# Attention on 32 graphs, one core: sums taken half a step earlier, output products and shares half a step later, paired negations, and the values' second copy issued from ACT's queue

## What is computed

```
q, k, v = (proj(Wq, bq), proj(Wk, bk), proj(Wv, bv))
scores = einsum('bhqd,bhkd->bhqk', q, k) * SCALE * (adj + adj)
attn = softmax(scores, axis=-1)
ctx = einsum('bhqk,bhkd->bhqd', attn, v)
out = layernorm(x + ctx @ Wo.T + bo)
```

## Time and profile before

| | us |
|---|---|
| median of 3 runs | 419.25 (416.65 to 419.89) |
| profiled execution, its time | 418.86 |
| its span | 416.3 |

### The profile page before, as it was taken

How to read it: one execution, slowest core, us unless ns; L and a number is a source line. 1 busy time by engine, 2 the same in 40 slices (tenths; PEclk the granted TensorE clock), 3 DMA queues, 4 the chain that set the end, 5 groups by cost and what they waited for, 6 DMA issues and landing times.

```text
span 416.3 us, 12182 instructions
## 1 busy us (share of the span) xinstructions
PE 382.1 (92%) x3628; PEld 291.4 (70%) x3628; DVE 386.2 (93%) x1592; ACT 361.6 (87%) x1223; POOL 249.6 (60%) x379
## 2 busy tenths in 40 slices
PE   8989999999996999999999999899999999997772
PEld 6766777777674877777777776677777777675542
DVE  4988999999997799999999999999999999999865
ACT  4699999989897798999999999889899999999560
POOL 3143557677573775748577575757758474555455
PEclk9999999999999899999999999999999999999898
DMA  8468889989988789889989888888999898888632
GB/s 272 131 173 238 236 201 254 245 237 247 244 237 234 191 223 244 244 243 251 253 237 246 241 237 235 230 242 233 248 245 248 227 232 208 219 234 183 144 105 76
DMA packets 65427, 92.29 MB, mean 222 GB/s; under 512 B 8529, under 2 KB 48722, under 8 KB 65362
## 3 DMA queue, kind: packets, MB, share of 16 engines
q1 hardware_dynamic: 47426, 66.35, 63.9%
q10 hardware_dynamic: 17936, 25.17, 18.0%
HBM read 26.22 MB, written 8.39 MB: 83 GB/s over the span
## 4 chain that ended last, share of the span: by engine, by line
DVE 33%; PE 28%; DMA 12%; SPq 11%; issue 9%; ACT 4%; POOL 1%; DVEq 0%; ACTq 0%; POOLq 0%
DVE boxes L540 15%; DVE probs L521 13%; SPq L208 9%; DMA v_boxed<-v 8%; PE ctx_bank L404 7%; PE out_bank L421 5%; PE proj_bank L333 5%; PE out_bank L351 4%; PE row_bank L264 3%; ACT probs L728 3%; DMA carried<-boxes 3%; PE turn_bank L281 2%; SPq L217 2%; DVE stats L567 1%; DVE low_top L530 1%
## 5 line engine op out<-in xcount | busy, mean ns | idle before, releaser
L728 ACT ACTIVATE probs<-probs,low_top 128x256 f32<-128x256 f32 x512 | 254.6, 504 | 12.1 <-DVE low_top L530 12.1
L521 DVE CUSTOM_DVE_ANT_0 probs<-row_bank,adj_rows 128x256 f32<-128x256 f32 x512 | 187.4, 414 | 6.7 <-PE row_bank L264 5.9
L540 DVE STREAM_TRANSPOSE boxes<-probs 128x1536 f32<-128x1536 f32 x62 | 109.6, 1768 | 0.0
L333 PE MATMUL proj_bank<-xt_parts,w_parts 128*128 128x512 f32 x360 | 99.2, 411 | 0.0
L728 ACT ACTIVATION_READ_ACCUMULATOR probs<-probs,low_top 128x1 f32 x512 | 99.1, 194 | 0.0
L333 PEld LDWEIGHTS proj_bank<-xt_parts,w_parts 128*128 128x128 f32 x360 | 62.9, 188 | 30.5 <-issue 19.9
L404 PE MATMUL ctx_bank<-carried,v_boxed 128*32 128x256 f32 x744 | 61.9, 392 | 18.3 <-DMA v_boxed<-v 12.2
L867 POOL COPY wide<-shares 128x512 f32<-128x512 f32 x32 | 19.5, 610 | 92.2 <-DVE shares L548 92.2
L264 PE MATMUL row_bank<-kq 32*128 32x256 f32 x1024 | 73.3, 400 | 0.5 <-DVE top L521 0.5
L404 PEld LDWEIGHTS ctx_bank<-carried,v_boxed 128*32 128x32 f32 x744 | 32.3, 111 | 43.4 <-issue 31.4
L264 PEld LDWEIGHTS row_bank<-kq 32*128 32x128 f32 x1024 | 46.3, 184 | 11.7 <-issue 6.4
(11 more groups left out here) (85 smaller groups left out, 461.1 us busy)
## 6 DMA issues: line engine op xcount, KB each, us to landing
carried<-boxes SPq DMA_DIRECT2D x248, 192.0 KB, 3.9
xt<-in_x_t SPq DMA_DIRECT2D x32, 256.0 KB, 3.5
adj_rows<-in_adj ACTq DMA_DIRECT2D x32, 256.0 KB, 4.8
xr<-in_x ACTq DMA_DIRECT2D x32, 256.0 KB, 3.8
v_boxed<-v SPq DMA_DIRECT2D x124, 64.0 KB, 3.0
out<-result ACTq DMA_DIRECT2D x31, 256.0 KB, 5.3
w_whole<-in_wk ACTq DMA_DIRECT2D x2, 128.0 KB, 3.7
w_whole<-in_wq SPq DMA_DIRECT2D x1, 256.0 KB, 4.3
```

The lines of the kernel that those rows point to most:

```text
L333: last = nc.tensor.matmul(proj_bank[:], w_parts[:, a, which, t, c * P:(c + 1) * P], xt_parts[:, pair % 2, b, t, :], start=(half_ == 0 and ...
L521: last = nc.vector.tensor_tensor_reduce(probs[:, h % RING, t * S:(t + 1) * S], row_bank[j][:, t * S:(t + 1) * S], adj_rows[:, (g // 2) % 2 ...
L540: nc.vector.transpose(boxes[:, n % BOXES].rearrange("p a h (f q) -> p (h f) a q", q=D), probs[:, first:first + BOXED, :].rearrange("p h (f ...
L728: last = nc.scalar.activation(tile, tile, ACT.Exp, bias=low_top[:, g % 2, J * c + j, t:t + 1], accum_out=sums[:, g % 2, t, j * T + c:j * T ...
```

## The change

- **ACT**: `carry_v` moves from SP's list to ACT's: for graph 0 in slot 2 of step 0, and for graph g+1 in slot 6 of step g, behind that slot's `exp`. `copy_v(g+1)` goes from slot 3 to slot 5, ahead of `move_turned(2g)`. `copy_inverse` is now of graph g-2 and stands ahead of the step's first `exp`. `load_masks` goes from slot 2 to slot 4. `store` is of graph g-5, not g-4. The values' landing is told by four semaphores instead of two.
- **PE**: in a step, `project_out` is of graph g-3 and stands with `turn_shares(g-2)` ahead of `weigh_v(g-2)` in the first half; `project_v(g+1)` moves from the first half to the end of the second, ahead of `turn_probs(2g)`. `project_out` and `turn_shares` leave the second half.
- **DVE**: the eight `lower_top` of a step become four `lower_tops`, each for two heads; the first of a group stands behind its third `reduce_rows`, the second behind its fourth. `add_residual` and `row_stats` are of graph g-3, `aggregate` of g-4; `scale_context(g-2)` goes from the step's middle, ahead of `box(2g-1)`, to behind it.
- **POOL**: `make_scale` and `normalise` are of graph g-4, and the steps' slots are arranged anew.
- Behind the last step more is left over: an output product, a set of shares, an aggregate and a normalisation.

```diff
@@ SP @@
-            def carry_v(n):
-                sp.wait_ge(v_ready, n + 1)
-                wait(sp, ctx_made, n - 3)
-                for j in range(J):
-                    sp.dma_start(v_boxed[j::J, (n // 2) % 2, n % 2].rearrange("p t e -> p (t e)"),
...
                 if 0 < g <= LAST:
                     carry_boxes(2 * g - 1)
-                if 0 <= g + 1 < LAST:
-                    carry_v(g + 1)
@@ PE @@
-                if g < B:
-                    rows(2 * g)
+                rows(2 * g)
                 if is_pair(ahead):
                     for half_ in range(2):
                         project_kq(ahead, 2 * (g % 2), half_)
                 if g == 1:
                     make_bias()
+                if is_graph(g - 3):
+                    project_out(g - 3)
                 if is_graph(g - 2):
+                    turn_shares(g - 2)
                     weigh_v(g - 2)
-                if is_group(2 * g - 1):
-                    turn_probs(2 * g - 1)
-                if is_graph(g + 1):
-                    project_v(g + 1)
-                if is_graph(g):
-                    rows(2 * g + 1)
+                turn_probs(2 * g - 1)
+                rows(2 * g + 1)
                 if is_pair(ahead):
                     for half_ in range(2):
                         project_kq(ahead, 2 * (g % 2) + 1, half_)
-                if is_graph(g - 1):
-                    turn_shares(g - 1)
-                if 0 <= g - 2 < LAST:
-                    project_out(g - 2)
-                if 0 <= g < LAST:
+                if is_graph(g + 1):
+                    project_v(g + 1)
+                if g < LAST:
                     turn_probs(2 * g)
@@ DVE @@
+            def lower_tops(n, half_):
+
+                g, place = n // T, J * (n % T) + 2 * half_
+                dve.wait_ge(rows_used, J * n + 2 * half_ + 2)
+                nc.vector.tensor_reduce(low_top[:, g % 2, place:place + 2, :], top[:, g % 2, place:place + 2, :].unsqueeze(3),
+                                        AXIS.X, ALU.max, negate=True).then_inc(top_ready, 2)
...
                 for j in range(J):
                     reduce_rows(n, j)
-                    if j > 0:
-                        lower_top(n, j - 1)
+                    if j == 2:
+                        lower_tops(n, 0)
                     if j == 1 and n % T == 0 and n > 0:
                         divide(n // T - 1)
-                lower_top(n, J - 1)
+                lower_tops(n, 1)
@@ ACT @@
+            def carry_v(n):
+
+                act.wait_ge(v_ready, n + 1)
+                wait(act, ctx_made, n - 3)
+                for j in range(J):
+                    act.dma_start(v_boxed[j::J, (n // 2) % 2, n % 2].rearrange("p t e -> p (t e)"),
+                                 v[D * j:D * (j + 1), (n // 2) % 2, n % 2].rearrange("p t e -> p (t e)")
+                                 ).then_inc(v_in[n % 4], 16)
...
+                    if s == 0 and is_graph(g - 2):
+                        copy_inverse(g - 2)
                     if is_group(n):
                         exp(n, j)
...
-                    if s == 2 and is_graph(g + 2):
+                    if s == 2 and g == 0:
+                        carry_v(0)
+                    if s == 6 and 0 <= g + 1 < LAST:
+                        carry_v(g + 1)
+                    if s == (4 if g > 0 else 2) and is_graph(g + 2):
                         load_masks(g + 2)
                     if s == 1 and is_group(2 * g - 1):
                         move_turned(2 * g - 1)
+                    if s == 5 and is_graph(g + 1):
+                        copy_v(g + 1)
                     if s == 6 and is_graph(g):
                         load_x(g)
-                    if s == (3 if g > 0 else 5) and is_graph(g + 1):
-                        copy_v(g + 1)
```

More of the change, by code:

```diff
@@ L102, in build @@
         biases_in = sem("biases_in")
-        stored, v_in = ([sem(f"{name}{n}") for n in range(2)] for name in ("stored", "v_in"))
-        x_in, adj_in, carried_in = ([sem(f"{name}{n}") for n in range(4)] for name in ("x_in", "adj_in", "carried_in"))
+        stored = [sem(f"stored{n}") for n in range(2)]
+        x_in, adj_in, v_in, carried_in = (
+            [sem(f"{name}{n}") for n in range(4)] for name in ("x_in", "adj_in", "v_in", "carried_in"))
         xt_in = [[sem(f"xt_in{n}_{t}") for t in range(T)] for n in range(2)]
@@ L229, in _ @@
                     load_x_t(pair, t)
-            carry_v(0)
             def step(g):
@@ L277, in turn_probs @@
                 wait(pe, moved, n)
-                wait(pe, inverted, n // 2)
+                wait(pe, inverted, (n + 1) // 2 - 1)
                 for t in range(T):
@@ L362, in turn_shares @@
                 else:
-                    pe.wait_ge(moved, 2 * g + 2)
+                    pe.wait_ge(moved, min(2 * g + 3, 2 * LAST))
                 for half_ in range(2):
@@ L373, in weigh_v @@
                 if g < LAST:
-                    pe.wait_ge(v_in[g % 2], 64 * (g // 2 + 1))
+                    pe.wait_ge(v_in[g % 4], 64 * (g // 4 + 1))
                 if g == 0:
@@ L497, in _ @@
                 step(g)
-            for c in range(T):
-                for j in range(J):
-                    turn_last(c, j)
+            turn_shares(LAST - 1)
+            for j in range(3):
+                turn_last(0, j)
+            project_out(LAST - 2)
+            for c, j in ((0, 3), (1, 0), (1, 1)):
+                turn_last(c, j)
             weigh_v(LAST - 1)
+            for j in (2, 3):
+                turn_last(1, j)
             turn_shares(LAST)
@@ L671, in step @@
                     nc.vector.tensor_copy(bias[:], ctx_bank[:, 0:E]).then_inc(bias_ready, 1)
-                if 0 <= g - 2 < LAST:
-                    scale_context(g - 2)
+                if is_graph(g - 3):
+                    add_residual(g - 3)
                 if is_group(2 * g - 1):
                     box(2 * g - 1)
[L676 to L682, removed]
+                if is_graph(g - 4):
+                    aggregate(g - 4)
+                if is_graph(g - 2):
+                    scale_context(g - 2)
+                mask_group(2 * g + 1)
+                if g < LAST:
                     box(2 * g)
-                if 0 <= g - 2 < LAST:
+                if is_graph(g - 3):
                     for t in range(T):
-                        row_stats(g - 2, t)
+                        row_stats(g - 3, t)
             for g in range(B):
                 step(g)
-            for c, j in ((0, 2), (0, 3), (1, 0), (1, 1), (1, 2)):
-                move_last(c, j)
+            aggregate(LAST - 3)
+            for j in (2, 3):
+                move_last(0, j)
+            add_residual(LAST - 2)
+            for j in (0, 1):
+                move_last(1, j)
+            for t in range(T):
+                row_stats(LAST - 2, t)
+            scale_context(LAST - 1)
             divide(LAST)
+            move_last(1, 2)
             aggregate(LAST - 2)
-            scale_context(LAST - 1)
             for half_ in range(2):
@@ L811, in step @@
                     n, j = 2 * g + s // J, s % J
+                    if s == 0 and is_graph(g - 2):
+                        copy_inverse(g - 2)
                     if is_group(n):
                         exp(n, j)
-                    if s == 0 and 0 <= g - 4 < LAST:
-                        store(g - 4)
+                    if s == 0 and is_graph(g - 5):
+                        store(g - 5)
                     if s == 0 and g == 0:
@@ L823, in step @@
                         move_turned(2 * g - 1)
+                    if s == 5 and is_graph(g + 1):
+                        copy_v(g + 1)
                     if s == 6 and is_graph(g):
                         load_x(g)
-                    if s == (3 if g > 0 else 5) and is_graph(g + 1):
-                        copy_v(g + 1)
                     if s == (3 if g > 0 else 4) and is_pair(ahead):
                         read_kq(ahead, 2 * (g % 2) + 1)
-                    if s == 3 and is_graph(g - 1):
-                        copy_inverse(g - 1)
+                    if s == 2 and g == LAST:
+                        copy_inverse(LAST - 1)
                     if s == 5 and 0 <= g < LAST:
@@ L841, in _ @@
             move_last(1, 3)
-            store(LAST - 3)
+            store(LAST - 4)
             copy_inverse(LAST)
@@ L845, in _ @@
                 high_last(half_)
-            for n in (LAST - 2, LAST - 1):
+            for n in (LAST - 3, LAST - 2, LAST - 1):
                 store(n)
@@ L924, in step @@
                 for s in range(H):
-                    if s == 0 and is_graph(g - 1):
+                    if s == 0 and g % 2 == 1 and is_pair(g // 2 + 2):
+                        cut_x(g // 2 + 2, 1)
+                    if s == 1 and is_graph(g - 1):
                         spread_shares(g - 1)
-                    if s == 1 and g % 2 == 1 and is_pair(g // 2 + 2):
-                        cut_x(g // 2 + 2, 1)
```

(9 more changed lines are left out.)

2 lines of the change are left out of this document (removed).

## The result

The changed kernel takes 524.84 us (median of 6 runs, 521.89 to 527.27) against 416.7 us for the one before in the same rounds: a ratio of 1.258 (95% interval 1.2515 to 1.2649). The direction was forecast; the forecast of 437 us and its range to 446 us were far too low. (The title speaks of sums taken half a step earlier. The diff leaves `weigh_v(g-2)` in the first half of its step, only behind `project_out` and `turn_shares`.)

The account below looks back on a forecast made before the run. ACT was taken to become the bound, at 12.70 us a step: 27.0 + 2 + 30 x 12.70 + 25.4 + 1 = 436.4 us of span, 439 us by the sum, taken as 437; own range 429 to 446 us.

Parts of the forecast that it names:

- the cover of 1.46 us: ACT's work in hand when the first issue starts: `move_turned` and the `exp` of slot 6, between `copy_v` and slot 7.
- the five: Four `carry_v` issues and `load_x` on ACT's queue before slot 7's `exp`: 2.4 us plus 0.58, 3.0 us together.
- A load of 0.33 us in the midst of an issue of SP: ACT's load during SP's 2.77 us issue stayed short, so no waiting for SP's issues was put in the sum.
- The rival with dearer issues: ACT's issues wait for SP's, 0.3 us more each: 4.2 us, stall 2.7, steps 13.9, 472 us in all; chance 0.07.
- The rule beside it, of a lock held by one queue at a time: The descriptor-making unit is locked for one queue at a time; cited for a still dearer issue, not put in the sum.
- ACT's step is then 11.15 + 1.55: ACT's work of 11.15 us plus its stall ahead of slot 7 of 1.55 gives a step of 12.70 us.
- `copy_inverse` fills most of the later start: On ACT, a group's first `exp` can start about 0.8 us later; `copy_inverse`, 0.46 us, fills most of that.
- The pairing: On DVE, two heads' negations in one instruction save 0.14 us a group, 0.28 a step: 11.64 becomes 11.36 us.
- PE's waits for blocks vanish, 11.6 us a step without the stall: PE's wait ahead of `weigh_v`, 18.2 us in all, goes; PE's floor stays 11.56 us, steps near 11.6 without stall.
- Ends: Outside the 30 steps: 2 us added in step 0 for two `carry_v`, 1 us behind the last step.
- the cheap issue: ACT's issues cost 0.335 us each, PE bounds at 11.56 us, steps of 11.65, 405.5 us in all; chance 0.15.
- the bounds: Issue prices on ACT from 0.335 to near 1.0 us per set's one issue: stall 0.4 to 1.95, ACT 11.55 to 13.1 us.

Follow-up runs that it names:

- experiment 1: The changed kernel with the values' second copy issued from SP again, as before the change: 422.31 us, 1.0129 of the kernel before.
- experiment 2: The kernel before with only the values' second copy moved to ACT's queue, slot 6, `copy_v` staying in slot 3: 437.59 us, 1.0483.
- experiment 10: The changed kernel with the burst in the same slot 6 but of graph g, whose `copy_v` was done a step earlier: 448.62 us, 1.0786.
- experiment 9: The changed kernel with SP's block copies moving 128 of each row's 1536 bytes, same number of issues: 493.52 us, 1.1877.
- experiment 7: The changed kernel with the values' four issues on ACT taken apart, one each in slots 6, 7, 1 and 2: 425.13 us, 1.0194.
- experiment 3: The changed kernel with DVE's `divide` moved behind the whole mask, values still issued from ACT: 509.21 us, 1.2157 of the kernel before.
- experiment 11: The changed kernel with the values' issues on ACT one each in slots 6, 7, 1 and 2, and negations for each head: 408.19 us, 0.9823.

## Why the prediction was right and wrong

- **Direction and place: right.** ACT's queue was named as what decides, with the wait behind `copy_v`, the cover of 1.46 us, and the idle time ahead of slot 7 put down to "issue". The cover is 4.59 - 3.14 = 1.45 us. Experiments 1, 2 and 10 show that this is the cause.
- **The length of the issues: the larger failed step.** The sum took 3.0 us for the five; 4.54 us were measured in the step shown (212.32 to 216.86). The first two took about what was predicted, 0.50 and 0.67 us in the mean for 0.47 and 0.60; the third and fourth 1.27 and 1.24 us in the mean, `load_x` 0.90 in the median in place of 0.58. The mean stall was 3.31 us a step in place of 1.55: 1.8 us of the missing 2.9 us a step (15.57 - 12.70). The prices were SP's own, taken while ACT's queue carried little; that the changed order puts the burst beside SP's blocks wasn't considered. A load of 0.33 us in the midst of an issue of SP was read as proof that the two don't touch. Experiment 9 shows that they do. The rival with dearer issues, 4.2 us for the five, was nearer in size, but its 0.3 us more for each had no row behind it. The rule beside it, of a lock held by one queue at a time (the Trainium skill, "Perfetto Trace Analysis", section "DMA Instruction — HWDGE"), no run here confirms as the cause: in experiment 7 issues beside one of SP were short. That the other queue's bytes matter is all that experiment 9 tells.
- **"ACT's step is then 11.15 + 1.55": the other failed step, in how the terms are added.** ACT's work and its stall were taken for the whole step. With the measured 3.3 us that rule gives 14.5 us and some 490 us in all, not 525. What stood behind `exp` 7 was listed as `box`, `turn_probs` and `read_kq`; `divide` was left out, though it waits for the eighth `exp` in the middle of DVE's masks. DVE then can't run ahead, `exp` 4 waits for it, and `copy_v`, which starts the burst, waits for `exp` 5. ACT's waits for DVE and PE are the missing 1.0 us a step; in experiment 3 the one for DVE is gone, and the step is 0.6 us shorter. By the loop, 10.83 us (15.42 - 4.59) plus the issues, the predicted 3.0 us would have given 13.8 us a step and some 470 us. So either failure alone puts the time above the range.
- **"`copy_inverse` fills most of the later start": wrong for the second group.** It stands ahead of `exp` 0. `exp` 4 has nothing ahead of it and waits 0.93 us in experiment 1. The pairing was booked as a gain of 0.28 us a step. DVE's work did fall, by 0.2 us a step after the change (11.68 to 11.47 us), but the pairing costs 13 us in the new order and 7 in the old.
- **PE's waits for blocks vanish, 11.6 us a step without the stall: right in kind.** 18.2 us became 0.9, and 1.4 in experiment 11, where no stall hides them. That run, with neither burst nor pairing, has steps of 11.60 us.
- **Ends.** 2 us were added at the start, 4.7 were found; 1 at the end, 1.2 were found. (The sum of 405.5 us for the cheap issue leaves out the 2 us; nothing hangs on it.)

The range held no case in which the stall comes back around: its highest rival needed a dearer issue, and the bounds moved only the issue's price, never the rule by which the terms are added.

## What to carry to other kernels

When a wait or a stall is put on an engine's list, follow what it releases until the chain comes back to where it began; if it comes back, the step can't be shorter than the way around, whatever idle time the engines have. In this kernel a DMA issue on a computing engine was free only while that engine had more in hand than the issue lasted. So place the issues singly, and put no set of them behind a wait for a result that the same engine has just made. Fewer instructions on the busiest engine are no gain if the first result comes later to an engine that has no work meanwhile.

## What the runs showed of the hardware

The length of an issue on ACT's queue rose with what SP's queue had to move: the set of four took 3.77 us beside full blocks and 2.83 us beside blocks of a twelfth of the bytes, while cutting the values' own bytes to a sixteenth gave 3.48 us. Why the third and fourth issue of experiment 7 take 0.95 and 1.02 us, though only 7 and 8 of 29 stand beside an issue of SP, while the first two stand beside one each time and take half as long, stays open.

PE's clock fell where PE had come to idle. The window rows of the two steps show 0.94 and 0.89 of the full clock after the change, against 1.00 before. Here PE had been idle for 2.44 us, waiting for `copy_inverse`; the 16 products of one group take 2.09 us right behind that wait and 1.15 us later in the step. The windows of these two stretches show a granted clock of 0.50 and 1.00 (third number from the end), its levels of 1.2 and 2.4 GHz:

```profile
203.70:206.80 3.10, 3.03 (x20) 1.94 (x20) 3.00 (x7) 3.10 (x12) 1.27 (x1) 0.50 0.25 85
210.50:213.10 2.60, 2.56 (x22) 2.01 (x23) 2.60 (x5) 2.60 (x10) 2.25 (x6) 1.00 1.00 285
```

The slower clock can explain little of the loss: of 109 us, DVE waits for scores 4.3 us in the whole run and ACT for `proj_bank` 10.6 us. Timeline of the changed kernel, PE:

```profile
203.77 1.09 PE L270 MATMUL turn_bank<-ident,probs 128*128 128x128 f32 x4 [2.44 <-ACT inverse L739]
204.79 2.09 PE L253 MATMUL row_bank<-kq 32*128 32x256 f32 x16
...
210.54 1.15 PE L253 MATMUL row_bank<-kq 32*128 32x256 f32 x16 [0.16 <-DVE top L511]
```
